# A recommender tower with a Compressed Interaction Network: the first tile's loads and weight sums reordered, and GpSimd's gathers placed in four spots

## What is computed

```python
e = stack([tbl_f[ids[:, f]] for f in range(39)], axis=1)        # 512 x 39 x 16
prev = x = e
for k in range(3):                                              # w0: 39*39 x 128, w1, w2: 39*128 x 128
    z = einsum('bmd,bhd->bdmh', x, prev).reshape(b, 16, m * h)
    t = transpose(z @ w[k] + bias[k], (0, 2, 1))
    prev = t = t / sqrt(sum(t * t, axis=(1, 2), keepdims=True))
    logit.append(t)
h = concat([concat(logit, 1).sum(-1), dense_ctx], 1)            # 384 + 16
y = relu(relu(h @ W1 + b1) @ W2 + b2) @ W3
```

## Time and profile before

| | |
|---|---|
| median of 3 runs | 1170.16 us (1168.98 to 1170.77) |
| profiled execution | 1173.38 us |
| its span | 1171.6 us |
| TensorE busy | 1120.3 us (96%) |
| VectorE busy | 994.8 us (85%) |
| GpSimd busy | 946.5 us (81%) |
| ScalarE busy | 144.6 us (12%) |
| mean granted TensorE clock | 0.991 |

### The profile page before, as it was taken

One profiled execution on the slowest core, in us unless ns is written; L12 is line 12 of the kernel. 1 busy time (PEld: TensorE's weight loads), 2 busy tenths in 40 slices (PEclk: granted clock), 3 DMA queues, 4 the chain that ended last, 5 costly groups with the idle time before them and its releaser, 6 DMA issues. The chain is left out here.

```text
span 1171.6 us, 22368 instructions
## 1 busy us (share of the span) xinstructions
PE 1120.3 (96%) x8252; PEld 612.8 (52%) x8252; DVE 994.8 (85%) x875; ACT 144.6 (12%) x298; POOL 946.5 (81%) x646
## 2 busy tenths in 40 slices
PE   0788999999999999999999999999999999999999
PEld 0344555555555555555555555555555555555553
DVE  2658989899898989989898998988999898999782
ACT  0001111101111110111111011111101011110102
POOL 5566889798888979898897989889798988958680
PEclk9898999999999999999999999999999999999999
DMA  6886637293653718275472827547282844728010
GB/s 181 252 273 222 200 104 265 67 320 92 241 181 127 251 65 328 75 261 161 143 245 68 318 71 270 152 152 247 72 303 71 284 138 168 236 69 300 1 51 1
DMA packets 102345, 205.81 MB, mean 176 GB/s; under 512 B 49915, under 2 KB 52923, under 8 KB 102326
## 3 DMA queue, kind: packets, MB, share of 16 engines
q1 hardware_dynamic: 95312, 203.29, 51.7%
q0 software_dynamic: 5120, 1.29, 1.1%
q10 hardware_dynamic: 1894, 0.96, 0.4%
HBM read 203.05 MB, written 2.46 MB: 175 GB/s over the span
## 5 line engine op out<-in xcount | busy, mean ns | idle before, releaser
L642 DVE TENSOR_TENSOR z<-t_ps,xb 128x2048 f32<-128x2048 f32 (+2 forms) x352 | 711.1, 2043 | 68.0 <-PE acc L822 43.5
L340 POOL TENSOR_TENSOR sums<-z,sums 128x1024 f32<-128x1024 f32 x224 | 531.6, 2373 | 53.8 <-DVE sums L655 38.7
L808 PE MATMUL acc<-z,w_sb 128*64 128x512 f32 x1408 | 327.6, 601 | 16.5 <-DVE z L642 10.7
L822 PE MATMUL mix_ps<-sums,s_sb 128*64 128x256 f32 x1792 | 330.8, 380 | 2.0 <-POOL sums L340 0.8
L337 POOL TENSOR_TENSOR sums<-z 128x512 f32<-128x512 f32 x192 | 245.7, 1280 | 83.6 <-DVE z L642 79.4
L822 PE MATMUL acc<-z,w_sb 128*64 128x256 f32 x896 | 269.4, 383 | 0.2
L822 PE MATMUL mix_ps<-z,w_sb 128*64 128x256 f32 x896 | 269.4, 383 | 0.0
L822 PE MATMUL acc<-z,s_sb 128*64 128x256 f32 x896 | 267.9, 381 | 0.0
L822 PE MATMUL p_ps<-z,w_sb 128*64 128x256 f32 x896 | 267.9, 381 | 0.0
L822 PEld LDWEIGHTS mix_ps<-sums,s_sb 128*64 128x64 f32 x1792 | 187.2, 137 | 99.3 <-POOL sums L340 13.5
L822 PE MATMUL acc<-sums,w_sb 128*64 128x256 f32 x896 | 230.9, 380 | 0.0
(11 more groups left out here) (80 smaller groups left out, 447.7 us busy)
## 6 DMA issues: line engine op xcount, KB each, us to landing
xb<-xt SPq DMA_DIRECT2D x128, 512.0 KB, 6.5
xb<-xq SPq DMA_DIRECT2D x112, 512.0 KB, 5.1
xb<-xt SPq DMA_DIRECT2D x48, 768.0 KB, 6.8
xr<-xt SPq DMA_DIRECT2D x47, 468.0 KB
x<-xt SPq DMA_DIRECT2D x15, 234.0 KB
xr<-xt SPq DMA_DIRECT2D x15, 234.0 KB
gathered<-in_table,rows_of POOLq DMA_INDIRECT x160
xt<-gathered SPq DMA_DIRECT2D x16, 72.0 KB, 2.3
```

Of the source, the lines that this page charges most:

```text
L340: nc.gpsimd.tensor_tensor(t41, b2, t2_twice, ALU.subtract).then_inc(t41_ready, 1)
L642: nc.vector.tensor_tensor(z[:, at:at + n, :], t_ps[k - 1][:, :].rearrange("p (a n) -> p a n", a=1).broadcast_to([P, n, N]), xb[:, XB_ROW[c ...
L808: last = nc.tensor.matmul(acc[k][o, :], w_sb[k][:, field + r, o], z[:, at + r, :], start=(c == 0 and r == 0), stop=(c == NCH - 1 and r == ...
L822: return nc.tensor.matmul(bank[side, cols], weights, moving, start=start, stop=stop, skip_group_check=True)
```

## The change

The program's layout of w1 and w2 in DRAM becomes one contiguous run per partition; both are loaded at the start of SyncE's list. The rows of tile 0 are written from ScalarE's queue. In tile 0, VectorE makes parts 0 and 1 of the summed weights of layer 2 behind the first group of `products0(0)`, parts 2 and 3 behind the products of chunks 3 and 4 of layer 1, and `products0(1)` where every other tile has it. The mixed rows of tile 1 are written after the layer 0 loads of tile 1. GpSimd's gathers go to four places.

```diff
-GATHERS_AFTER = {(1, LAST_P): (0, 7), (2, 6): (7, 8), (2, LAST_P): (8, 10)}
+GATHERS_AFTER = {(1, 5): (0, 1), (1, 6): (1, 2), (1, LAST_P): (2, 8), (2, LAST_P): (8, 10)}
...
+        def write_rows(engine, i):
...
+                engine.dma_start(blk, gathered[0:fields * TILE_B, g0:g1, :]).then_inc(xt_written, 16)
...
-            sp.dma_start(w_sb[1][:, :, :], w1.rearrange("(m h) o -> h m o", h=P)).then_inc(w_loaded[1], 16)
-
-            def write_rows(i):
...
+            sp.dma_start(w_sb[1][:, :, :], w1).then_inc(w_loaded[1], 16)
+            sp.dma_start(w_sb[2][:, :, :], w2).then_inc(w_loaded[2], 16)
...
-            write_rows(0)
             write_mixed(0)
             sp.wait_ge(xt_written, 48)
 
...
                 load_chunk(0, c)
                 if c == NCH // 2:
 
-                    write_rows(1)
-                    write_mixed(1)
-            sp.dma_start(w_sb[2][:, :, :], w2.rearrange("(m h) o -> h m o", h=P)).then_inc(w_loaded[2], 16)
+                    write_rows(sp, 1)
             sp.wait_ge(xt_written, 96)
             sp.wait_ge(acc0_ready, 1)
             load_layer0(1)
+            write_mixed(1)
...
             act.wait_ge(bias_loaded, 48)
 
+            write_rows(act, 0)
             act.wait_ge(xt_written, 48)
...
-                    if c == NCH - 2 and first:
-                        mixed_weights(2, 0)
-                    if c == 9 and not first and not last:
+                    if first and c in (3, 4):
+                        mixed_weights(2, c - 1)
+                    if c == 9 and not last:
                         products0(i + 1, (0, 1, 2,))
-                    if c == 10 and not first and not last:
+                    if c == 10 and not last:
                         products0(i + 1, (3,))
-                if first:
-
-                    products0(i + 1, range(len(LOADS0)))
-                    for part in range(1, 4):
-                        mixed_weights(2, part)
...
-            products0(0, range(len(LOADS0)))
+            products0(0, (0,))
+            for part in range(2):
+                mixed_weights(2, part)
+            products0(0, range(1, len(LOADS0)))
...
+    def by_unit(w):
+        return np.ascontiguousarray(w.reshape(FIELDS, UNITS, UNITS).transpose(1, 0, 2))
...
-        "w1": a["L0_rec_w1"], "w2": a["L0_rec_w2"], "b0": a["L0_rec_b0"], "b1": a["L0_rec_b1"],
+        "w1": by_unit(a["L0_rec_w1"]), "w2": by_unit(a["L0_rec_w2"]), "b0": a["L0_rec_b0"], "b1": a["L0_rec_b1"],
```

More of the change, by code:

```diff
@@ L279, in load_shifted, with write @@
             engine.dma_start(xr[:, k0:k1, :].rearrange("p k n -> p (k n)"), src).then_inc(xr_loaded[g], 16)
+        def write_rows(engine, i):
+            def write(first, g0, g1, fields=GROUP):
+                blk = xt[bass.ds(i, 1), first:first + (g1 - g0 - 1) * GROUP + fields, :].rearrange(
+                    "a (g f) (b d) -> (a f b) g d", f=fields, d=EMB)
+                engine.dma_start(blk, gathered[0:fields * TILE_B, g0:g1, :]).then_inc(xt_written, 16)
+            engine.wait_ge(rows_gathered, 16 * (GROUPS - 1) * (i + 1))
+            write(0, 0, GROUPS - 1)
+            write(FIELDS, 0, (XT_ROWS - FIELDS) // GROUP)
+            engine.wait_ge(last_gathered, 16 * (i + 1))
+            write((GROUPS - 1) * GROUP, GROUPS - 1, GROUPS, LAST_GROUP)
         block = ctx.enter_context(nc.Block())
@@ L443, in _ @@
                 load_fields(i)
-                write_rows(i + 1)
+                write_rows(sp, i + 1)
                 write_mixed(i + 1)
```

## The result

The changed kernel takes **1165.01 us** (median of 8 runs, 1162.17 to 1166.31) beside 1170.41 us for the kernel before (8 runs, 1168.98 to 1173.04). The ratio is 0.9943, with a 95% interval from 0.9931 to 0.9955: 6.7 us less (5.3 to 8.1), faster. The two medians alone lie 5.4 us apart, at the lower end of that. In a second batch the changed kernel had 1164.54 us and 0.9936 [0.992, 0.9951]. The forecast was 1160.3 us, in a range from 1155.5 to 1165; the median lies at the upper end of it. The profiled execution took 1164.92 us, near the median, with a span of 1163.1 us: 8.5 us less than the profiled one of before (1171.6), which was 3 us above its own median.

A forecast was written before the change was run, and what follows sets the result against it. TensorE, busy 96% of the span, bounds the kernel; only its idle or slow time in tile 0 can be won. -14.35 + 3.1 + 1.4 = -9.85 us, from 1170.16 to 1160.3 us, range 1155.5 to 1165.

The forecast's parts named there:

- the 14.35 us: Tile 0 behind layer 1's last pairs: TensorE's idle time and slow clock from VectorE's wait for w2, all won back.
- Layer 0's loads for tile 1: Loads for products0(1): there at 67 to 69 us, ahead of VectorE at 70.0; cost nothing, cover about a microsecond.
- the wait goes elsewhere: Rival: layer 0's loads for tile 1 come late, some 4 to 9 us of 14.35 stay, about 1167 us; chance 0.07.
- Parts 2 and 3, 3.1 us: Weight sums between chunks 3 and 5 of tile 0: VectorE and GpSimd lock one another out, costing 3.1 us.
- no hindrance: Rival: weight sums slip between GpSimd's operations and the start costs next to nothing, 1156.6 us; chance 0.25.
- The start, 1.4 us: Start of tile 0: weight sums beside the last gathers 0.7 us, rows' write beside w2's end 0.7 us.
- the other 0.7: Start of tile 0: rows written beside the end of w2, nothing to about 2.6 us, taken as 0.7.
- w2 holds up the start: Rival: longer pieces don't raise the rate, w2 lands at 27 us and delays the start, 1164.9 us; chance 0.15.
- the comfort I took: DMA engines take queues in turn, packet by packet, so ScalarE's queue gets tile 0's rows past w2.
- GpSimd's gathers, nothing: New gather places in GpSimd's waits of each tile: nothing, between 1.4 us more and 1.4 less over 14 tiles.
- GpSimd becomes the bound of each tile: Rival: slower gathers at the new places cost 1.3 us in each of 14 tiles, 1178 us; chance 0.05.
- that the median lies 3.2 us below a profiled execution: Last step, from profiled execution to median: 1173.38 us becomes 1170.16, and 1163.5 becomes 1160.3.

The follow-up runs named there:

- e11: The changed kernel with parts 2 and 3 of layer 2's weight sums in VectorE's pause before layer 1, a repeat of e2; 1162.30 us, ratio 0.9918.
- e2: The changed kernel with parts 2 and 3 of layer 2's weight sums moved into VectorE's pause between products0(0) and the first norm; 1161.62 us, ratio 0.9912.
- e10: The changed kernel measured again, on the same chip as e11; 1164.54 us, ratio 0.9936.
- e4: As e2, and SyncE waits for the gathers of tile 0 before it issues w2; 1164.07 us, ratio 0.9929.
- e5: The changed kernel with w2's last 15 fields loaded behind tile 0's xr loads and all four weight-sum parts in the pause; 1161.36 us, ratio 0.9909.
- e8: The changed kernel with all of w2 behind tile 0's xr loads, ahead of xb, and all four weight-sum parts behind products0(0); 1163.35 us, ratio 0.9925.
- e9: As e5, but w2 in three pieces of 16, 14 and 9 fields, the last behind tile 1's layer 0 loads; 1160.3 us, ratio 0.9906.
- e1: The changed kernel with GpSimd's gathers back at their old three places; 1164.42 us, ratio 0.9932.
- e6: The changed kernel with w1 and w2 in 512-byte pieces as before, both still loaded at the start; 1169.06 us, ratio 0.997.
- e7: The changed kernel with tile 1's mixed rows written back in the middle of the xb loads, ahead of chunk 6; 1166.11 us, ratio 0.9951.

## Why the prediction was right, and where not

**What bounds the kernel, and the 14.35 us: right.** TensorE goes from the last pairs of layer 1 of tile 0 through layer 0 into layer 2 without an idle time, at 2.4 GHz. From the last pairs' start to the sum two tiles on it is 220.91 - 81.95 = 138.96 us, where a steady tile had 139.11: 14.50 us are won. Of these the late start takes 3.95 back, and layer 1 as far as that matmul takes 34.58 us instead of 32.42, 2.16 more: -14.50 + 3.95 + 2.16 = -8.39, the distance between the two sums. Layer 0's loads for tile 1 cost nothing, as forecast, but the cover was thinner than worked out: in e11 they came at 72.5 to 76.6, not at 67 to 69, and VectorE had to wait for them. The rival "the wait goes elsewhere" is right about the place that comes next.

**Parts 2 and 3, 3.1 us: right, and by the mechanism named.** Its rival (no hindrance) is refuted by the rows of 3.90 and 1.99 us, and by e2. Moved away they give 2.7 us from start to sum. Against the kernel before only 2.16 show, because that one was itself slower than e2 in layer 1: 24.30 us from the start to chunk 9's products, not 23.79. It had waited for a load of `xb`:

```profile
59.41 3.96 DVE L642 TENSOR_TENSOR z<-t_ps,xb 128x2048 f32<-128x2048 f32 x2 [0.34 <-DMA xb<-xt]
```

The slow clock at the head of layer 1 is not it. e10 had it for longer than the changed kernel (granted clock 0.50 from 50 to 54 us, where the other had 0.81), and both needed the same 37.7 us.

**The start, 1.4 us: this step failed,** in size and in mechanism. I put 0.7 us on gathers whose *issue* would take longer beside layer 1's weight sums. The last one took 0.97 us. What grew was the *landing* of their rows, 4.66 us instead of 1.47, beside w2's traffic, which ran until 20 us; e4, e5, e8 and e9 show in steps that less of w2 means less delay. How the gathers and w2 share the DMA engines is not shown. The rows' write, forecast at 19 to 20 us, was issued at 21.89, when w2 had landed: the write took 3.35 us (to 25.24) against 2.97, 0.4 us instead of the other 0.7. The start cost 3.4 us at this point and 3.95 at the first product. In e1 it was 1.9 us, but there layer 0's 20 matmuls ran in 4.51 us, which took 6.76 in the kernel before and 6.21 in the changed one. The rival "w2 holds up the start" had the right place and the wrong reason: the rate rose to 412 GB/s and w2's traffic ended at 20, not 27. That the median came out at this rival's 1164.9 us is chance. And the comfort I took from the Trainium skill's rule (DMA: Bandwidth & Descriptors, section on queues, rings and completion order: an engine takes the queues in turn, packet by packet) did not hold as I read it. In e4 ScalarE's queue had one part of the rows' write, 6 KB, beside w2 on SyncE's: it did not get past w2, but took 8.3 us instead of 1.8. That the engines take turns isn't refuted by this; each turn may cost a long packet, but no run here counts the turns.

**GpSimd's gathers, nothing: right** (e1). The rival on the other side, that GpSimd becomes the bound of each tile, is out with it: 67.89 us per tile in both.

**The median.** For the profiled execution the forecast was 1163.5 us, and it took 1164.92, 1.4 us more: the start's term was 2.55 too small, the parts' 0.94 too large, and the 14.35 were 0.15 more. The other 3.3 us of the 4.7 between 1160.3 and 1165.0 come from one further step: that the median lies 3.2 us below a profiled execution. For the kernel before that was so in its first runs. It had 1171.9 to 1172.3 in three later batches, on three chips, so that the first median was a low one, and beside those the changed kernel gains 7.7 to 7.8 us (e10, e1). The changed kernel's profiled execution was at its median. Why the medians of one kernel move by 2 us is open: the chip is one candidate, and the slow matmuls of layer 0 in tile 0, which differ between executions of the same program (e2 and e11), are another; no run here isolates either. Of the forecast gain of 9.85 us, 6.7 to 7.8 were measured. That it is not less is partly luck: the parts' term erred the other way than the start's. (The range's lower end is a slip: 1156.6 - 1.4 is 1155.2, not 1155.5.)

## What to carry to other kernels

Giving a late transfer an earlier place moves it in front of something: price what small-piece transfers (gathers, writes of short rows) do while it runs, by their landing and not by their issue, and keep as much of it as can wait behind them (e5, e9). VectorE work with two SBUF inputs belongs where GpSimd is waiting for something else. And the layout alone, one line per matrix, won 5 us, about two thirds of what the whole rework won: take such parts singly before crediting the reordering. Last, a profile is one execution. Look where its time lies among the runs before you explain a median by it (e6).

## What the runs showed of the hardware

- 2.56 MB in pieces of 512 bytes moved at 278 GB/s, in one run per partition at 412 GB/s, both with the DMA engines busy throughout; issuing the second such transfer of short pieces blocked SyncE's queue for 9.95 us, of long pieces 0.44 us or less.
- Beside such a transfer on another queue, the rows of the last gathers landed 4.66 us behind the last gather's end instead of 0.19 to 0.29 us; 6 KB of 64-byte pieces, issued together with it, took 8.3 us to land instead of 1.8 (e4). Beside the last 4 us of a transfer in 512-byte pieces the whole write of such rows took 7.0 us instead of 3.0 (e6). Short pieces suffer from either sort of neighbour.
- Two engines that hinder one another both pay: a weight sum of 1.16 us took 3.90, 3.91, 3.89, 3.90 and 3.32 us in five profiles (the changed kernel, e1, e6, e7, e10), and a T2 of 1.28 us took 1.98 or 1.99 us. Two such parts cost the chain 2.7 us.
- A matmul of layer 0 lasted from 592 to 1116 ns in e10 while the granted clock read 1.00 throughout. The granted clock of a row doesn't explain every slow matmul.
